# A graph stack on one core: Pool's gather transfers on four semaphores instead of two, with a wait before every fourth

## The reference, cut to what matters

```python
h = maximum(layernorm(x), 0)
x = x + layer(h, adj)
```

```python
vals = where(valid[..., None], x[:, None, :, :], big)
sv = sort(vals, axis=2)
for tau, wt in zip(TAUS, QWEIGHTS):
    pos = clip(tau * (m - 1.0), 0.0)
    q = gather(floor(pos)) * (1.0 - frac) + gather(ceil(pos)) * frac
    agg = agg + wt * q
```

## Time and profile before

| | us |
|---|---|
| median of 3 executions | 2498.13 |
| lowest and highest of them | 2496.76, 2528.07 |
| the profiled execution | 2528.18 |
| its span, first to last instruction | 2526.3 |

### The profile page before, as it was taken

One profiled execution on the slowest core, in us unless ns is written; L12 is line 12 of the kernel. 1 busy time (PEld: TensorE's weight loads), 2 busy tenths in 40 slices (PEclk: granted clock), 3 DMA queues, 4 the chain that ended last, 5 costly groups with the idle time before them and its releaser, 6 DMA issues.

```text
span 2526.3 us, 48127 instructions
## 1 busy us (share of the span) xinstructions
PE 1538.7 (61%) x20741; PEld 1202.0 (48%) x20789; DVE 1718.8 (68%) x2475; ACT 470.4 (19%) x868; POOL 1336.5 (53%) x1190
## 2 busy tenths in 40 slices
PE   2665567575766757666765767576665756674303
PEld 2544345454554545454554645455454635454203
DVE  1544767858677786958677686957767695766534
ACT  3230211303021220302121120302112030210000
POOL 1036663646556564655656455654656465565630
PEclk9777657777776776677776768666676777766555
DMA  3231231313122231323222131412223131111110
GB/s 96 68 82 28 43 70 26 85 21 92 21 53 59 32 84 21 93 24 73 37 52 65 28 85 22 93 21 51 59 29 86 20 76 21 23 21 24 20 17 5
DMA packets 106545, 121.62 MB, mean 48 GB/s; under 512 B 71326, under 2 KB 71454, under 8 KB 106270
## 3 DMA queue, kind: packets, MB, share of 16 engines
q0 software_dynamic: 36864, 37.82, 13.1%
q1 hardware_dynamic: 69406, 79.95, 10.6%
HBM read 109.23 MB, written 8.45 MB: 47 GB/s over the span
## 4 chain that ended last, share of the span: by engine, by line
DVE 38%; PE 28%; issue 12%; DMA 8%; another core or an unknown queue 8%; ACT 4%; POOL 1%; DVEq 1%; POOLq 0%; ACTq 0%; SPq 0%
PE ps_prod L592 10%; DMA slots<-h_rows,row_no 8%; DVE slots L971 7%; DVE slots L970 4%; PE ps_misc L815 4%; PE ps_misc L579 4%; DVE lists L1147 3%; PE ps_tr L571 2%; PE ps_misc L768 2%; ACT h_t L435 2%; PE ps_key L663 1%; PE ps_key L667 1%; DVE xc L951 1%; DVE stat L950 1%
## 5 line engine op out<-in xcount | busy, mean ns | idle before, releaser
L399 POOL DMA_INDIRECT slots<-h_rows,row_no x1152 | 1326.1, 1151 | 1093.4 <-DMA slots<-h_rows,row_no 521.1
L592 PE MATMUL ps_prod<-mid,adj_t 128*128 128x64 bf16 x3584 | 476.3, 210 | 38.8 <-issue 37.6
L592 PE MATMUL ps_prod<-low,adj_t 128*128 128x64 bf16 x3584 | 475.7, 210 | 31.9 <-issue 31.3
L592 PEld LDWEIGHTS ps_prod<-mid,adj_t 128*128 128x128 bf16 x3584 | 377.3, 110 | 52.7 <-issue 51.6
L592 PEld LDWEIGHTS ps_prod<-low,adj_t 128*128 128x128 bf16 x3584 | 377.2, 110 | 45.8 <-issue 44.5
L592 PE MATMUL ps_prod<-y,adj_t 128*128 128x64 bf16 x2688 | 348.4, 208 | 27.1 <-issue 26.8
L592 PEld LDWEIGHTS ps_prod<-y,adj_t 128*128 128x128 bf16 x2688 | 277.6, 108 | 35.1 <-issue 34.8
L970 DVE TENSOR_TENSOR slots<-slots 128x1280 f32<-128x1280 f32 (+1 forms) x96 | 196.7, 2049 | 120.3 <-issue 112.2
L1147 DVE MAX8 lists<-ps_key 128x8 f16<-128x1024 f32 x128 | 157.8, 1233 | 60.9 <-PE ps_key L667 43.7
L971 DVE TENSOR_TENSOR slots<-slots 128x1280 f32<-128x1280 f32 (+1 forms) x96 | 195.9, 2041 | 0.0
L571 PE MATMUL ps_tr<-ident_f,h 128*64 128x128 f32 x256 | 59.9, 414 | 220.2 <-DVEq L1301 191.8
(11 more groups left out here) (210 smaller groups left out, 3652.3 us busy)
## 6 DMA issues: line engine op xcount, KB each, us to landing
adj_f<-in_adj SPq DMA_DIRECT2D x128, 512.0 KB
slots<-h_rows,row_no POOLq DMA_INDIRECT x1152
x<-in_x SPq DMA_DIRECT2D x16, 256.0 KB
h_rows<-h SPq DMA_DIRECT2D x16, 256.0 KB
out<-x SPq DMA_DIRECT2D x16, 256.0 KB
y<-in_L_gnn_W SPq DMA_DIRECT2D x1, 64.0 KB
w_sb<-in_L_gnn_W SPq DMA_DIRECT2D x2, 32.0 KB
h_rows<-zeros SPq DMA_DIRECT2D x2, 32.0 KB, 1.5
```

The source lines that it names most:

```text
L399: pool.indirect_dma_start(out=slots[:, slot_of(par, s), t * C:(t + 1) * C], out_offset=None, in_=table[par][:, :], in_offset=bass.Indirect ...
L592: last = nc.tensor.matmul(ps_prod[:, t * C:(t + 1) * C], block_t, part(j), start=(j == 0 and k == 0), stop=(j == T - 1 and k == 2))
```

## The change

There are four semaphores per parity instead of two, and the transfers go over them in turn. The wait now stands before every transfer on lane 0, so before every fourth, and looks at lane 2 (LANES - 2), the third of the four preceding transfers. 72 transfers are 18 per lane. DVE's loop over the lanes at L1265 now waits for four semaphores, each for 18 transfers of 16 per graph of its parity instead of 36.

```diff
-    LANES = 2
+    LANES = 4
...
                 def row(column, s, t):
                     one = gathered[par][issued[0] % LANES]
                     if issued[0] % LANES == 0:
-                        at_least(pool, one, (issued[0] // LANES) * 16)
+                        at_least(pool, gathered[par][LANES - 2], (issued[0] // LANES) * 16)
```

## The result

| | kernel before, us | changed kernel, us |
|---|---|---|
| median | 2505.91 (2496.76 to 2528.07, 4 runs) | 2894.14 (2877.05 to 2912.9, 4 runs) |
| profiled execution, span | 2526.3 | 2911.1 |

The ratio is 1.154, 95% interval 1.143 to 1.165: the change makes the kernel 15% slower. I had forecast 2486.4 us within 2473 to 2517, and given slower by over 2% a chance of 0.02. The forecast was wrong by 408 us and in its sign.

What follows compares the result with a forecast made beforehand. No single bound: DVE waits for the gather at fill and drain; DVE and PE pace the middle turns. From 2498.1 us, -10.2 - 3.1 + 1.6 = -11.7 gives 2486.4 us; own range 2480 to 2492, full range 2473 to 2517.

Steps and rivals of the forecast that it cites:

- Waits removed: On Pool, 18 of a gather's waits go; in the drain, DVE's wait for graph 15's gather shrinks by 10.2 us.
- landing as a latency: Gather transfers still land 2.86 us after their start with more in flight, so each remaining wait keeps its length.
- the fill: Graph 0's gather, before the first sort: DVE's wait falls from 7.11 to about 4.1 us, gaining 3.1 us.
- Five in flight instead of three: Assumption for Pool's gather queue: five transfers overlap after the change, and landing time holds; not shown by the trace.
- Waits added to DVE: Ahead of each turn's sort, two more semaphores at 0.05 us each over 16 turns: +1.6 us, range 0 to +3.5.
- The middle turns: The 14 turns between fill and drain: gather done before DVE comes, so a faster gather gains 0.
- denser issue beside DVE: Gather instructions beside DVE's sorting steps: Pool pays for the overlap, DVE doesn't; taken as 0 for DVE.
- C: Rival: landing time grows with transfers in flight, lengthening each gather by 11 us; +48, 2546 us; chance 0.05.
- D: Rival: denser gathers hold up DVE's sorting steps through the shared port, +14 us, 2501 us; chance 0.02.
- A: Rival: the transfer queue is a rate, so removed waits return in the next one; 2499.7 us; chance 0.13.
- B: Rival: all of Pool's waiting in the gather falls away, 21.3 us in the drain; 2475.3 us; chance 0.08.
- E: Rival: the run lies in the upper part of the earlier spread, 2516.5 us median, gain unchanged; chance 0.10.

Runs made afterwards that it cites:

- e2: Changed kernel's new waits (before every fourth transfer) with only two semaphores per parity, as in the kernel before; 2896.1 us, ratio 1.140.
- n4: Kernel before without the gathers of graphs 4 to 15, in a set that starves PE; 2299.5 us, ratio 0.924.
- e6: Changed kernel with eight semaphores, up to nine transfers allowed in flight, in a set without starving; 2268.8 us, ratio 0.969.
- e7: Changed kernel fetching rows of 64 instead of 256 bytes from graph 3 on, in a set without starving; 2274.1 us, ratio 0.972.
- r1: Same edit of the changed kernel as e7, in another set without starving; 2276.5 us, ratio 0.970.

## Why the prediction was wrong

*The gather's own times: right.* Waits removed (10.2 us forecast in the drain, 48.6 - 39.0 = 9.6 measured ahead of the sort), landing as a latency (1.16 to 1.24 us per wait), the fill's 7.11 to 4.24. The sum of the gains that I had worked out was there, about 12 us.

*Five in flight instead of three: a wrong reading that did no harm to the sum.* By my own cadence, 1.245 us per transfer and 2.86 us until it lands, three overlap at most; the traces have 1.79 on average against 1.60. The assumption that landing would hold was therefore hardly tested, and it held (2.80 us at the median against 2.84).

*Waits added to DVE: too high.* The 14 middle waits come to 99.6 - 39.0 - 4.2 = 56.4 us, 4.03 each, where they were 4.04. Two more satisfied semaphores cost nothing that shows; my +1.6 us should have been 0.

*The failed step: "The middle turns are paced by DVE and PE waiting for each other ..., and a faster gather gives them nothing."* They were put at nothing, and each got 26 us longer, the kernel 388 us. I treated the gather as something that others can only wait for. It is also something that others suffer from: in the starting profile PE's gaps inside products stood at 139.5 us in 299, L1205 waited 181.2 us for PE, and a part of the chain was "another core or an unknown queue" (8%). I read L1205's wait as the ordinary pace of the turn and never asked why a product of L592, which takes 5.8 us at its quickest, took 10.2 us at the median and up to 19.3 us. For "denser issue beside DVE" I weighed only DVE as the neighbour that could pay, and by the one rule that I knew; PE was not on the list.

*The rivals.* C was the slower one, and its condition did not hold: landings did not grow. It had the wrong victim, and from that the wrong price, +48 instead of +388. D did not happen either: the longest L970 is 2.83 us, before 2.88, so the trace shows again only Pool behind DVE, and a denser gather did not bring out the other half of the rule that I had quoted there. A and B are settled by the halved waits. E was a hint that I undervalued: it was 1.3% between executions of one kernel, and five sets later the spread between sets of runs is 8.6% (2339.5 to 2540.4). Most of it goes with the gathers: without them the two kinds of sets are 36 us apart.

*What stays open.* Shown: gaps without a wait inside PE's products; the new waits alone bring them (e2), semaphores and rows do not, and they go when the gathers go (30.1 us left in n4, all but 3.0 of it where it still gathers); they grow as the gather is issued more densely; three of five sets of the experiments and the result show them, two don't. Not shown: whether the rate or the overlap of the transfers counts, by which way they hold PE up, and what makes a set of one kind or the other. Two sets ran on the chip with the same number and were of different kinds, so it is not simply the chip.

A late supply of instructions is a rival for the way. The Trainium skill (Runtime: NRT & Kernel Launch, Instruction fetch mechanics) says that the instruction memory of an engine is refilled in blocks of 16 KiB by a DMA queue of its own, and that crossing a block is mostly hidden. The queues of the page show these blocks, in the changed kernel as in the one before:

```profile
q0 software_dynamic: 36864, 37.82, 12.4%
...
q8 instruction: 195, 3.19, 0.5%
```

195 packets with 0.5% of the engines' time in both, so the transfers of instructions themselves are not slower. Nor are they late in most gaps. Between 1244 and 1264 us, where PE stands again and again, the only queue with packets is this one:

```profile
q0 software_dynamic: 477, 0.49, 20.7%
```

The last refill before began at 1242.04. Over the whole changed kernel 720 gaps of 0.5 to 4 us lie between neighbouring instructions of PE on ps_prod, and a packet of q8 ends in only 23 of them (counted in the trace). So nearly all of these gaps have another cause than a late refill; at which point PE is held no run here shows. The changed kernel itself did not run in a set without starving either; that it would gain about 3% there is argued from e6, e7 and r1, which are denser gathers of the same kind.

No version beats both kernels everywhere. Where PE is starved, two allowed in flight has the lowest ratio (0.982, in one set and not clear of 1), and where it is not, the denser gathers (0.969 with nine allowed, against 1.210 in the other kind).

## What to carry to other kernels

A queue that is off the critical path can slow the engine that is on it; before making it denser, look for gaps "<- issue" inside runs of instructions that have nothing to wait for, and whether they come only while that queue is at work. Leaving out the suspected traffic altogether is the cheapest measurement of what it already costs: here it showed 150 us in a kernel whose gather looked free. And the number of transfers that the waits allow is a setting to be measured in more than one set of runs, with the kernel before beside it each time, since what nine allowed did changed sign between sets. What the waits allow is not what is in flight: count that in the trace before reasoning with it.

## What the runs showed of the hardware that I had not expected

- Beside densely issued gather transfers PE stood for about 1.03 us after every four or five matmuls, with no wait, down to 62 matmuls in 18 us; DVE's sort steps kept their 2.83 us.
- At one granted clock (0.50) a product went at 71 matmuls in 4 us and, a few microseconds later, at 62 in 18 us.
- Of the gather transfers only two or three overlap (1.89 on average where nine are allowed), since one is issued per 1.25 us and is through after 2.8 us. Half the rows per transfer did not help (510.1 us of gaps).
- Refills of instructions do not coincide with the gaps: 23 of 720.
- The same kernel took 2339.5 us in one set of runs and 2540.4 us in another, with scatter of 0.2% and 1.1% within them, and without gathers nearly the same in both kinds (2263.2 and 2299.5 us).
- Satisfied waits on two more semaphores did not show on DVE (4.03 against 4.04 us).
